# RWKV layer with an int32-weight FFN: weights cast to bf16 by the DMA instead of by ScalarE and VectorE

## What is computed

```python
xn = layernorm(x)
# attention (RWKV): C = 1024
k = xn @ Wk.T ; r = xn @ Wr.T ; v = r
y = wkv_scan(-exp(time_decay), time_first, k, v)   # a recurrence along the tokens
a = (sigmoid(r) * y) @ Wo.T
# feed-forward on the same xn: HIDDEN = 3072, weights stored as int32 in -127..127
wg, wu, wd = w_gate / 127, w_up / 127, w_down / 127
f = (silu(xn @ wg.T) * (xn @ wu.T)) @ wd.T
out = x + a + f
```

## Time and profile before

| | |
|---|---|
| Median of 2 runs | 2048.27 us (2045.66 to 2050.88) |
| The profiled execution's own time | 2044.83 us |
| Its span on the slowest core | 2043.3 us (cores: 2030.7 to 2043.3) |
| TensorE busy | 1484.2 us, 73% of the span |
| VectorE busy | 845.2 us, 41% |
| ScalarE busy | 388.0 us, 19% |
| DMA, mean over the span | 66 GB/s |

### The profile page before, as it was taken

How to read it: one execution, slowest core, us unless ns; L and a number is a source line. 1 busy time by engine, 2 the same in 40 slices (tenths; PEclk the granted TensorE clock), 3 DMA queues, 4 the chain that set the end, 5 groups by cost and what they waited for, 6 DMA issues and landing times.

```text
span 2043.3 us, 18028 instructions; the slowest of 8 cores (2030.7 to 2043.3 us)
## 1 busy us (share of the span) xinstructions
PE 1484.2 (73%) x6368; PEld 631.6 (31%) x6368; DVE 845.2 (41%) x1403; ACT 388.0 (19%) x645; POOL 21.5 (1%) x28
## 2 busy tenths in 40 slices
PE   1254646556564747405668999999999999999997
PEld 0121222222121313102223444444444444444443
DVE  2287878787878776713331111111111111111111
ACT  2341414242323233200000110101101011010110
POOL 0000000000000000000000000000000000000000
PEclk8686968787777878758788999999999999999998
DMA  6510303030303010176661202002020020200201
GB/s 194 156 41 0 103 1 103 1 103 1 103 1 103 1 62 13 54 231 199 194 191 46 83 1 102 2 21 83 1 85 19 21 83 1 74 30 21 83 1 42
DMA packets 49785, 135.39 MB, mean 66 GB/s; under 512 B 2592, under 2 KB 10784, under 8 KB 49696
## 3 DMA queue, kind: packets, MB, share of 16 engines
q1 hardware_dynamic: 39072, 92.29, 14.6%
q0 software_dynamic: 10624, 41.94, 5.8%
HBM read 92.28 MB, written 41.94 MB: 66 GB/s over the span
## 4 chain that ended last, share of the span: by engine, by line
PE 46%; DMA 8%; DVE 2%; issue 1%; DVEq 0%; SPq 0%; POOL 0%; POOLq 0%
PE psB_gu L673 15%; PE psB_gu L681 15%; PE psB_d L710 9%; PE psB_d L694 7%; DMA stg<-wgT 3%; DMA stg<-wuT 3%; DMA stg<-wdT 2%; DVE pb L636 1%; DVE wubf L618 0%; DVE wgbf L618 0%; PE psB_d L701 0%; DVE wdbf L618 0%; DVE pb L643 0%; DVE h_act L628 0%; POOL out_cm L721 0%
## 5 line engine op out<-in xcount | busy, mean ns | idle before, releaser
L673 PE MATMUL psB_gu<-xnb,wgbf 128*128 128x512 bf16 x1536 | 370.5, 385 | 64.5 <-DVE wubf L618 64.5
L628 DVE SCALAR_TENSOR_TENSOR h_act<-psB_gu,silu 128x512 bf16<-128x512 f32 x192 | 132.7, 691 | 612.8 <-PE psB_gu L681 612.8
L681 PE MATMUL psB_gu<-xnb,wubf 128*128 128x512 bf16 x1536 | 364.3, 380 | 0.0
L658 ACT ACTIVATE silu<-psB_gu 128x512 f32<-128x512 f32 x192 | 114.7, 597 | 954.2 <-PE psB_gu L673 954.2
L694 PE MATMUL psB_d<-h_act,wdbf 128*128 128x512 bf16 x736 | 192.9, 385 | 55.6 <-DVE wdbf L618 31.7
L673 PEld LDWEIGHTS psB_gu<-xnb,wgbf 128*128 128x128 bf16 x1536 | 152.3, 99 | 252.3 <-issue 76.2
L681 PEld LDWEIGHTS psB_gu<-xnb,wubf 128*128 128x128 bf16 x1536 | 150.9, 98 | 183.0 <-issue 3.2
L710 PE MATMUL psB_d<-h_act,wdbf 128*128 128x512 bf16 x768 | 178.4, 397 | 22.5 <-DVE pb L636 22.5
L450 PE MATMUL ps_wo<-outpre,wo_bf 128*128 128x512 bf16 x448 | 117.9, 423 | 92.3 <-DVE xn_buf L404 77.9
L465 PE MATMUL ps_k<-xn_buf,wk_bf 128*128 128x512 bf16 x512 | 134.3, 410 | 43.1 <-ACT k_sb L203 32.1
L474 PE MATMUL ps_r<-xn_buf,wr_bf 128*128 128x512 bf16 x512 | 121.8, 381 | 0.0
(11 more groups left out here) (117 smaller groups left out, 971.8 us busy)
## 6 DMA issues: line engine op xcount, KB each, us to landing
x_buf<-x_cm SPq DMA_DIRECT2D x8, 2048.0 KB, 11.3
pt_scr<-x_buf POOLq DMA_DIRECT2D x8, 2048.0 KB, 8.7
pb<-pt_scr SPq DMA_DIRECT2D x8, 2048.0 KB, 8.7
out_cm<-pb POOLq DMA_DIRECT2D x8, 2048.0 KB, 8.4
stg<-wgT SPq DMA_DIRECT2D x24, 512.0 KB, 4.4
stg<-wuT SPq DMA_DIRECT2D x24, 512.0 KB, 4.3
stg<-wdT SPq DMA_DIRECT2D x24, 512.0 KB, 4.2
xn_scr<-xn_buf POOLq DMA_DIRECT2D x8, 1024.0 KB, 11.2
```

Of the source, the lines that this page charges most:

```text
L628: ve.scalar_tensor_tensor(out=h_act[:, hg * TC:(hg + 1) * TC], in0=up_sl(hg), scalar=1.0 / 127.0, in1=silu[hg % 2], op0=Alu.mult, op1=Alu. ...
L658: sc.activation(out=silu[hg % 2], in_=gate_sl(hg), func=Act.Silu, scale=1.0 / 127.0).then_inc(sem["s_sil"], 1)
L673: ins = te.matmul(gate_sl(hg), wgbf[:, gc * HID + hg * D:gc * HID + (hg + 1) * D], gsl(xnb, gc), start=(gc == 0), stop=(gc == G - 1))
L681: ins = te.matmul(up_sl(hg), wubf[:, gc * HID + hg * D:gc * HID + (hg + 1) * D], gsl(xnb, gc), start=(gc == 0), stop=(gc == G - 1))
```

## The change

The cast moves into the DMA. In stage one GpSimd issues three DMAs, one for each of Wk, Wr and Wo, that read float32 in HBM and write bf16 into SBUF; the staging buffers, the 24 loads of SyncE and the 24 casts of ScalarE are gone. SyncE loads x chunks 0, 1 and 2 at once at the start. GpSimd then issues twelve more casting DMAs, two ahead of the `xn_scr` write of each of the chunks 0 to 5: they read a piece of an int32 weight in HBM (3.1 MB) and write it as bf16 (1.6 MB) into new scratches `wg_bfd`, `wu_bfd`, `wd_bfd` in HBM. `ph` also waits for them. In stage two SyncE issues six plain bf16 loads (3.1 MB each, 18.9 MB in all) from these scratches into `wgbf`, `wubf`, `wdbf`, and only then the loads of `xnb` and `pb`; the 72 tile loads and VectorE's 72 casts are gone, and TensorE waits for the six loads.

```diff
@@ stage one, SyncE
-                for jj in range(2):
+                for jj in range(3):
                     sy.dma_start(
                         out=x_buf[jj].rearrange("p (g t) -> p g t", t=TC),
                         in_=hbm_chunk(x_hbm, jj)).then_inc(sem[f"sA_x{jj % 3}"], 16)
-                for i in range(24):
-                    if i >= 2:
-                        sy.wait_ge(sem["s_wcast"], i - 1)
-                    sy.dma_start(out=wstage[i % 2],
-                                 in_=w_tiles[i][0]).then_inc(sem[f"s_wload{i % 2}"], 16)
-                sy.wait_ge(sem["s_wcast"], 24)
-                sy.dma_start(
-                    out=x_buf[2].rearrange("p (g t) -> p g t", t=TC),
-                    in_=hbm_chunk(x_hbm, 2)).then_inc(sem["sA_x2"], 16)
@@ stage one, ScalarE (the same for i in range(16, 24) further down)
-                for i in range(16):
-                    sc.wait_ge(sem[f"s_wload{i % 2}"], 16 * (i // 2 + 1))
-                    sc.copy(out=w_tiles[i][1], in_=wstage[i % 2]).then_inc(sem["s_wcast"], 1)
@@ stage one, TensorE
-                        te.wait_ge(sem["s_wcast"], 16)
+                        te.wait_ge(sem["g_wk"], 16)
+                        te.wait_ge(sem["g_wr"], 16)
...
-                            te.wait_ge(sem["s_wcast"], 24)
+                            te.wait_ge(sem["g_wo"], 16)
@@ stage one, GpSimd
-                for j in range(NCH):
+                gp.dma_start(
+                    out=wk_bf.rearrange("p (g n) -> p g n", n=1024),
+                    in_=wk_hbm.rearrange("(g p) n -> p g n", p=D)).then_inc(sem["g_wk"], 16)
...
+                fpieces = []
+                for r in range(4):
+                    fpieces.append((wg_bfd[r * 256:(r + 1) * 256, :],
+                                    wg_hbm[r * 256:(r + 1) * 256, :]))
...
+                for j in range(NCH):
+                    for pc in range(2 * j, min(2 * j + 2, len(fpieces))):
+                        gp.dma_start(out=fpieces[pc][0],
+                                     in_=fpieces[pc][1]).then_inc(sem["g_fc"], 16)
                     gp.wait_ge(sem["v_xn"], j + 1)
                     gp.dma_start(
                         out=hbm_chunk(xn_scr, j),
...
+                gp.wait_ge(sem["g_fc"], 16 * 12)
                 gp.sem_inc(sem["ph"], 1)
@@ stage two, SyncE
                 sy.wait_ge(sem["ph"], 1)
...
+                sy.dma_start(
+                    out=wgbf.rearrange("p (g n) -> p g n", n=HID)[:, :, 0:1536],
+                    in_=wg_bfd.rearrange("(g p) n -> p g n", p=D)[:, :, 0:1536],
+                ).then_inc(sem["g_wgb"], 16)
...
+                sy.dma_start(
+                    out=wdbf.rearrange("p (g n) -> p g n", n=1024)[:, 12:HG, :],
+                    in_=wd_bfd.rearrange("(g p) n -> p g n", p=D)[:, 12:HG, :],
+                ).then_inc(sem["g_wdb2"], 16)
+                for j in range(NCH):
                     if j >= 1:
                         sy.wait_ge(sem["t_u"], 24 * j)
                     sy.dma_start(
...
-                    if j == 0:
-                        for i in range(20):
-                            load_w(i)
@@ stage two, VectorE
-                cast_w(20)
...
-                        cast_w(3)
@@ stage two, TensorE (chunk 0 alone; the same with g_wub and g_wdb)
-                            te.wait_ge(sem["v_fcast"], GATE_RDY[hg // 8])
+                            if hg < 12:
+                                te.wait_ge(sem["g_wgb"], 16)
+                            else:
+                                te.wait_ge(sem["g_wgb2"], 16)
```

More of the change, by code:

```diff
@@ L100, in build_nc @@
         wo_bf = sA.enter_context(nc.sbuf_tensor("wo_bf", [D, G * 1024], BF16)).ap()
[L101 to L105, removed]
         x_buf = [sA.enter_context(nc.sbuf_tensor(f"x_buf{i}", [D, G * TC], F32)).ap()
-                 for i in range(2)] + [x_buf2]
+                 for i in range(3)]
         xn_buf = [sA.enter_context(nc.sbuf_tensor(f"xn_buf{i}", [D, G * TC], BF16)).ap()
@@ L135, in gsl @@
             return ap_[:, g * w:(g + 1) * w]
[L137 to L143, removed]
         with nc.Block() as blk:
@@ L509, in _ @@
             def _(gp):
+                gp.dma_start(
+                    out=wk_bf.rearrange("p (g n) -> p g n", n=1024),
+                    in_=wk_hbm.rearrange("(g p) n -> p g n", p=D)).then_inc(sem["g_wk"], 16)
+                gp.dma_start(
+                    out=wr_bf.rearrange("p (g n) -> p g n", n=1024),
+                    in_=wr_hbm.rearrange("(g p) n -> p g n", p=D)).then_inc(sem["g_wr"], 16)
+                gp.dma_start(
+                    out=wo_bf.rearrange("p (g n) -> p g n", n=1024),
+                    in_=wo_hbm.rearrange("(g p) n -> p g n", p=D)).then_inc(sem["g_wo"], 16)
+                fpieces = []
+                for r in range(4):
+                    fpieces.append((wg_bfd[r * 256:(r + 1) * 256, :],
+                                    wg_hbm[r * 256:(r + 1) * 256, :]))
+                for r in range(4):
+                    fpieces.append((wu_bfd[r * 256:(r + 1) * 256, :],
+                                    wu_hbm[r * 256:(r + 1) * 256, :]))
+                for r in range(4):
+                    fpieces.append((wd_bfd[r * 768:(r + 1) * 768, :],
+                                    wd_hbm[r * 768:(r + 1) * 768, :]))
                 for j in range(NCH):
+                    for pc in range(2 * j, min(2 * j + 2, len(fpieces))):
+                        gp.dma_start(out=fpieces[pc][0],
+                                     in_=fpieces[pc][1]).then_inc(sem["g_fc"], 16)
                     gp.wait_ge(sem["v_xn"], j + 1)
@@ L532, in build_nc @@
         wdbf = sB.enter_context(nc.sbuf_tensor("wdbf", [D, HG * 1024], BF16)).ap()
-        stg = [sB.enter_context(nc.sbuf_tensor(f"stg{i}", [D, 1024], I32)).ap()
-               for i in range(2)]
         xnb = sB.enter_context(nc.sbuf_tensor("xnb", [D, G * TC], BF16)).ap()
@@ L541, in build_nc @@
         psB_d = sB.enter_context(nc.psum_tensor("psB_d", [D, 4 * TC], F32)).ap()
[L543 to L569, removed]
         def gate_sl(hg):
@@ L581, in _ @@
                 sy.wait_ge(sem["ph"], 1)
[L583 to L587, removed]
+                sy.dma_start(
[3 more added lines that the diff above has]
+                sy.dma_start(
+                    out=wubf.rearrange("p (g n) -> p g n", n=HID)[:, :, 0:1536],
+                    in_=wu_bfd.rearrange("(g p) n -> p g n", p=D)[:, :, 0:1536],
+                ).then_inc(sem["g_wub"], 16)
+                sy.dma_start(
+                    out=wdbf.rearrange("p (g n) -> p g n", n=1024)[:, 0:12, :],
+                    in_=wd_bfd.rearrange("(g p) n -> p g n", p=D)[:, 0:12, :],
+                ).then_inc(sem["g_wdb"], 16)
+                sy.dma_start(
+                    out=wgbf.rearrange("p (g n) -> p g n", n=HID)[:, :, 1536:HID],
+                    in_=wg_bfd.rearrange("(g p) n -> p g n", p=D)[:, :, 1536:HID],
+                ).then_inc(sem["g_wgb2"], 16)
+                sy.dma_start(
+                    out=wubf.rearrange("p (g n) -> p g n", n=HID)[:, :, 1536:HID],
+                    in_=wu_bfd.rearrange("(g p) n -> p g n", p=D)[:, :, 1536:HID],
+                ).then_inc(sem["g_wub2"], 16)
+                sy.dma_start(
+                    out=wdbf.rearrange("p (g n) -> p g n", n=1024)[:, 12:HG, :],
+                    in_=wd_bfd.rearrange("(g p) n -> p g n", p=D)[:, 12:HG, :],
+                ).then_inc(sem["g_wdb2"], 16)
                 for j in range(NCH):
-                    if j == 1:
-                        for i in range(20, NFT):
-                            load_w(i)
                     if j >= 1:
@@ L678, in _ @@
                         if j == 0:
-                            te.wait_ge(sem["v_fcast"], UP_RDY[hg // 8])
+                            if hg < 12:
+                                te.wait_ge(sem["g_wub"], 16)
+                            else:
+                                te.wait_ge(sem["g_wub2"], 16)
                         for gc in range(G):
@@ L688, in _ @@
                             if j == 0:
-                                te.wait_ge(sem["v_fcast"], DOWN_RDY[ph_hg])
+                                if ph_hg < 12:
+                                    te.wait_ge(sem["g_wdb"], 16)
+                                else:
+                                    te.wait_ge(sem["g_wdb2"], 16)
                             if ph_hg == 0 and j >= 1:
```

15 lines of the change are left out of this document (7 added, 8 removed).

## The result

The changed kernel takes 1965.8 us (median of 11 runs) against 2047.0 for the kernel before (10 runs beside them); the ratio is 0.9603, with a 95% interval of 0.9592 to 0.9614. That is 81 us less. 1975 was forecast, with a range of 1940 to 2012. Its profiled execution took 1964.4 us with a span of 1962.6 on the slowest core, here core 1. In some executions the cores of one die show a lower granted clock and take longer; the ratios, and the times given for the experiments, leave these out.

A forecast was written before the change was run, and what follows sets the result against it. The prediction took waits for weight loads and casts at the starts of both stages as the bound; -19 and -54 make -73 us from 2044.83, 1972, given as 1975 because the median stands 3.4 higher; range 1940 to 2012.

The forecast's parts named there:

- Stage two: From ph to the end of chunk 0: bulk loads replace tile loads and casts, 54 us less, bounds 47.5 to 72.
- the load: Start of stage two: 19.9 MB, six weight loads and xnb, at 290 GB/s take 69 us, 71 with landing.
- Low clock: First 16 matmuls of stage two: TensorE leaves idle at the low clock, 6.2 us instead of 3.5, 2.7 more.
- 127.5 us per chunk: Stage two: the time of a chunk without loads, taken for chunk 0; later chunks keep 127.5 to 129 us.
- that VectorE's casts give nothing of their own: Stage two: the 72 removed casts lay beside the waits for loads, so removing them adds no gain.
- Stage one, the start: Start through the first scan group: no ScalarE casts ahead of layernorm, 19 us less; bounds 37 gain to 12 loss.
- t0: When TensorE starts the first projection in stage one, set by x chunk 1's landing: 75.2 us; gain is 94.5 - t0.
- The price of a cast: Casting DMAs: a cast packet costs the same as a plain one; rival that it costs twice, 2006 us, chance 0.18.
- The pieces: Stage one: two pieces ahead of each xn_scr write take 24 to 31 us, hidden in 58.9 us of room.
- the rival of the other sign: Stage one: pieces outrun their cover, VectorE waits for xn_scr behind two pieces; 2161 us at 90 GB/s, chance 0.11.
- the prediction's own formula: VectorE's wait per stage-one chunk: time of the pieces plus 11 us for the queue, less 58.9 us of room.
- the sentence on the x loads: Stage one: x loads that meet pieces in the other queue take some 10 us more, with over 40 of room.

The follow-up runs named there:

- run with plain copies: Changed kernel with Wk copied as float32 by two plain DMAs instead of one cast, wk_bf zeroed; x chunk 1 squared at 46.1 us mean against 43.6.
- run with four pieces: Changed kernel with four pieces ahead of the xn_scr writes of chunks 1 to 3, instead of two for chunks 0 to 5; 2005.6 us, ratio 0.9785.

## Why the prediction was right

- **Stage two** was forecast as 71 us from `ph` to the first matmul, 201 to the end of chunk 0, 54 us less. It was 66.4 and 196.9 on the slowest core, and 56.4 less in the mean. The term that was too large is the load: from 854.5 to 916 us the eight cores moved 317 to 327 GB/s, not 290. The 358 GB/s that the Trainium skill (HBM Reference, Specifications) gives as effective per core stands above every core here. The two differ, and the measured rates decide. Low clock and 127.5 us per chunk came as forecast: the first 16 matmuls took 6.3 us, and chunk 0 ended 130.5 behind the first matmul (130.2 forecast). One sentence does not fit the trace of before, though the sum does not rest on it: that VectorE's casts give nothing of their own. The chain of before from 874 to 1131 us by line:

```profile
by line: DMA stg<-wgT 24.0%; DMA stg<-wuT 19.9%; DMA stg<-wdT 16.2%; PE psB_d L710 9.3%; PE psB_gu L673 6.7%; PE psB_gu L681 4.8%; PE psB_d L694 3.9%; DVE wubf L618 3.3%; DVE wgbf L618 3.3%; DVE wdbf L618 3.0%; issue 2.8%; DVE pb L636 1.0%;
```

  60% lie in loads into `stg`, and 9.6%, some 25 us, in the casts L618. No run separates the halved bytes from the vanished casts.
- **Stage one, the start** was forecast as t0 = 75.2 and 19 us less; it was 70.7 on the slowest core, and 23.4 less at the first scan group. The chain from L250 to `v_xn` took 20.8, as forecast, and x chunk 1 was squared at 45.0 instead of 50. The packets of 14 to 45 us (changed kernel, slowest core):

```profile
q0 software_dynamic: 1661, 3.36, 67.7%
q1 hardware_dynamic: 1660, 3.33, 38.7%
```

  1661 cast packets against 1660 of x: the counts agree with the turns by packet that the argument was built on and that the Trainium skill (DMA: Bandwidth & Descriptors, Queues, rings and completion order) states. A cast packet counts with its 2 KB written and stands for 4 KB read. So 6.7 MB and 3.3 MB were read in 31 us, 324 GB/s. From 5 to 14 us it was 267 (0.61 MB of casts as written, 1.18 MB of x), close to the 264 that the forecast had from the same window of the kernel before. That this rate was taken for the whole stretch is the mis-sized term; by 45 us 12.6 MB had been read, as the sum had it. The price of a cast, for which a plain packet's was taken, was right by the run with plain copies.
- **The pieces** were forecast as hidden, with 24 to 31 us for two of them and `xn_scr` landing 35 to 42 after its issue, in 58.9 us of room. It landed 41.4 to 42.8 us after it (chunks 1 to 5, slowest core), and VectorE never waited at the squaring. The run with four pieces shows the mechanism named as the rival of the other sign: the `xn_scr` write came some 14 us too late, 12 by the prediction's own formula, though the x load came later still. Wrong was the sentence on the x loads: not 10 us more but 23 (34.4 to landing instead of 11.3). The run with four pieces gives the room that hid it: an x load issued at 324.0 was wanted at 370.9, 47 us later.
- **Additive parts** were assumed and not examined. On the changed kernel the sum is right, 23 and 56, but the stage-two part without the stage-one part loses 27 of its 56 us, which the prediction would not have told.
- The sum was 73 for 80, both terms some 2 to 4 us short and of one cause: the rates taken for long loads leaned on the row of the first microseconds, and the loads went at 317 to 327 GB/s.

## What to carry to other kernels

When a load moves to the front of a stage, look at what stands behind it in its queue: the small tensor that the first instruction needs goes first, and the weights after it in the order and the slices in which they are used (here 50 us of a 66 us wait). The large background transfers cost these kernels nothing by their bytes; they cost through the transfers that they held up, in their own queue and in others; find for each of these who waits for its landing, and how much room there is. And a part of a change that costs nothing in one setting may do so only because another part removed what it would have collided with; run the parts alone before they are reused alone.

## What the runs showed of the hardware that was not expected

- A DMA from HBM to HBM with whole rows went in very large packets. In 206 to 216 us of the changed kernel, slowest core:

```profile
q0 software_dynamic: 32, 1.05, 94.3%
```

  That is 33 KB written, 66 KB of int32 read, for each packet. Once the x load flows, the other queue gets one packet of 2 KB for each (48 to 48 from 216 to 226 us). Two tiles of 0.5 MB took 32 us beside such pieces instead of 4.
- SyncE was held at its own DMA issues. An issue took 0.37 us with the queue empty, but in the chain of the changed kernel the third to sixth load of stage two take 9.18, 12.46, 6.46 and 9.41 us:

```profile
853.54 9.18 SPq L556
862.76 12.46 SPq L560
875.27 6.46 SPq L564
881.77 9.41 SPq L568
```

  Together 37.5 us in which SyncE issued nothing else. That the issues advance with the transfers ahead of them fits these rows but was not tested. It cost nothing here, as the DMA engines were busy all the time (share 0.99 from 854.5 to 916).
- A cast from float32 to bf16 in the DMA had no price of its own that these runs can see. For int32 no plain copy was run beside it; a piece moved some 105 GB/s as written, 210 as read (206 to 216 us, above).
